# Deformable convolution on one core: in the last batch every second interpolated tile is added up by TensorE

## The chip, the core and the metric

The kernel runs on one core of a Trainium2 chip. The metric is the device time of one execution in microseconds (us). The engines are TensorE (PE, its weight loads are shown apart as PEld), VectorE (DVE), ScalarE (ACT), GpSimd (POOL) and SyncE (SP); 16 DMA engines move data between HBM and the on-chip memory (SBUF), and TensorE writes its results to PSUM.

## The reference

The input is x with 8 images of 256 channels and 64 x 64 pixels, all float32. Two layers follow each other, each with a residual:

```
x = x + L0(gn(x))        # attention in a 3x3 neighbourhood with dynamic kernels, projection
x = x + L1(gn(x))        # modulated deformable 3x3 convolution
```

The change touches L1 alone. For every pixel and every one of the 9 taps a small convolution gives an offset and a mask. The sampled value is a bilinear mix of four corners with the mask folded in, and a 256 x 256 matrix for each tap contracts the channels:

```
v = samp(y0, x0) * ((1-ly)*(1-lx)) + samp(y0, x0+1) * ((1-ly)*lx)
  + samp(y0+1, x0) * (ly*(1-lx)) + samp(y0+1, x0+1) * (ly*lx)
v = v * mask
out = einsum('bckhw,ock->bohw', v, w)
```

## The kernel before, in words

**Tiles of the convolution.** An image is cut into 8 chunks of 512 pixels (8 rows). A unit is one chunk with one tap, 72 units an image. A unit has 4 tiles of 128 pixels, taken as 2 pairs, so an image has 144 pairs or 288 tiles (`PAIRS` = 144). Tiles are numbered through all images as `a`, pairs as `M = b * PAIRS + m`, and `a = 2 * M` or `2 * M + 1`. For each tile the engines do this:

- POOL (L762) gathers 128 rows of 1024 floats from a table in HBM into `G[a % 10]`. Each row holds the four corners of a pixel, 256 channels each. The gather waits until VectorE is done with tile `a - 10` (L761, `lerp[2]`).
- The first corner is scaled by its weight in place: ACT at L1131 in the stretches in which the front part of the next image runs its attention layer and in the last image, otherwise DVE at L1394.
- DVE adds the other three corners, each with one multiply-add (`scalar_tensor_tensor`): L1407 takes corners 0 and 1 into `V[a % 6]`, L1414 adds corner 2 and then corner 3. The two tiles of a pair alternate, so a pair is 6 instructions. Before them DVE waits until PE has turned pair `M - 3` (L1396).
- PE (L988) turns the tile, pixels on partitions to channels on partitions, by 4 transposes of 128 x 128 a pair, into one PSUM bank. It waits for `lerp[2]` (L985).
- ACT (L1142) copies the bank to `VT[U % 2]`, which holds a whole unit.
- PE (L781, `contract`) multiplies `VT` by the tap's weights into the two accumulators `CV[0]` and `CV[1]` (PSUM): 2 matmuls of 512 columns each time, once a pair (first half of the output channels of unit u - 1 at the second pair, second half of unit u - 2 at the first pair).
- After the ninth tap of a chunk DVE (L1198) adds each accumulator to the residual in `R`, SP stores `R` and loads the next one. PE waits for that add before it writes the accumulator again (L777).

**Order.** The order of the work is one written list (`order_of_steps`), and every engine runs its own share of the list in that order; semaphores alone tie the engines. While image b is convolved, the front part of image b + 1 (attention, projection, offsets, table) is laid between the pairs. The last image has no front part beside it. For a pair m the list has: lerp m (DVE), turn m - 1 (PE contracts, then transposes; ACT evacuates; DVE adds a residual where one is due), the gathers of two tiles, scale m + 2 (ACT). So ACT's evacuation of pair m - 1 stands in its queue before the scales of pair m + 2.

**Buffers and counters.** `E[0..5]` are six buffers of 1024 floats for the front part's products and table rows; the last image's convolution does not use them. `lerp[0]`, `lerp[1]` and `lerp[2]` count the tiles after their first, second and third multiply-add. `act_scale` counts ACT's scales, and `scale_counts` works out for each tile which count it has to wait for.

Of the kernel before, what the change touches and what calls it, by code (L numbers as in the profile page):

```python
# [13 lines left out]
P = 128  # L14
# [413 lines left out]
    return [(0, slot, n)] + ([(n, 0, 4 - n)] if n < 4 else [])  # L428


def scale_counts(steps):


    out, n = {}, {True: 0, False: 0}
    for s in steps:
        if s[0] == "scale":
            for i in range(2):
                n[s[3]] += 1
                out[2 * (s[1] * PAIRS + s[2]) + i] = (s[3], n[s[3]])
    return out  # L440


def build(nc, x, wqk, wv, wn, wkx, bkg, alpha, beta, wproj, woff, boff, wconv,
# [1 line left out]
    NB = x.shape[0]  # L445
    steps = order_of_steps(NB)
    banks, prods = rotations(steps)
    scaled = scale_counts(steps)
    ctx = ExitStack()
    with ctx:  # L450
        def sb(name, shape, dt=F32):
# [181 lines left out]
        def rows_of(g, i):  # L633

            n = len(table_blocks(g % NCH)[i])
            return E[prods.place["tt", g, i // 2]][:, CH * (i % 2):CH * (i % 2) + C * n]

        def norm_parts(j, b):

            if j == 1:  # L640
                return 2 + b, mv, gnt, gn2[b % 2]
            part = slice(0, 2) if b == 0 else slice(2, 2 * NB)
            return b, mv1[:, part, :], gnt1[:, :, part], gn1[:, :, part]
# [93 lines left out]
        @block.gpsimd  # L737
        def _(e):
            e.wait_ge(d_first, 16 * NFIRST)
            e.partition_broadcast(s_ab[:, :], row[0:1, 0:36]).then_inc(bcast, 1)  # L740
            e.partition_broadcast(s_bo[:, :], row[0:1, 36:63]).then_inc(bcast, 1)
            e.partition_broadcast(s_al[:, :], row[0:1, 63:65]).then_inc(bcast, 1)

            for s in steps:
                kind = s[0]
                if kind == "gather":
                    b, lo, hi = s[1:]
                    for n in range(lo, min(hi, 2 * PAIRS)):
                        u, i = divmod(n, 4)
                        c, t = unit(u)  # L750
                        a = 2 * PAIRS * b + n
                        col = column(b, c, i, t)
                        if n == 0:
                            e.wait_ge(d_zero, 64)
                            e.wait_ge(st1_done, 16 * NB)
                            for k in range(NE_BUF):
                                need_rows(e, k, NCH * (b + 1) - 1)
                        if n % 36 == 0:
                            e.wait_ge(wts, WTS * (b * NCH + c + 1))
                        if a >= NG:  # L760
                            e.wait_ge(lerp[2], a - NG + 1)  # L761
                        e.indirect_dma_start(  # L762
                            G[a % NG][:, :], None, T[b % 2],
                            bass.IndirectOffsetOnAxis(ap=IDX[:, col:col + 1], axis=0)).then_inc(d_g[a % NG], 16)

        @block.tensor
        def _(e):
# [17 lines left out]
            for s in steps:  # L785
# [189 lines left out]
                elif kind == "turn" and s[2] >= 0:  # L975
                    b, m = s[1:]
                    u, pair = divmod(m, 2)
                    M = b * PAIRS + m
                    if u > 1 and pair == 0:
                        contract(1, b, u - 2)  # L980
                    elif u > 0 and pair == 1:
                        contract(0, b, u - 1)
                    use = ("vt", M)
                    need_bank(e, use)
                    e.wait_ge(lerp[2], 2 * M + 2)  # L985
                    for n in range(2):
                        for h in range(2):
                            mm = e.transpose(BK[banks.place[use]][:, 2 * P * h + P * n:2 * P * h + P * n + P],  # L988
                                             V[(2 * M + n) % NV][:, h * P:(h + 1) * P], s_ident[:, :])
                    mm.then_inc(filled(use)[0], 1)  # L990
                elif kind == "conv.end":
                    b = s[1]
                    contract(1, b, UNITS - 2)
                    contract(0, b, UNITS - 1)
                    contract(1, b, UNITS - 1)

        @block.scalar
        def _(e):
# [29 lines left out]
            for s in steps:  # L1028
# [92 lines left out]
                elif kind == "scale" and s[3]:  # L1121
# [5 lines left out]
                    for i in range(2):  # L1127
                        a = 2 * (b * PAIRS + m) + i
                        col = column(b, c, 2 * pair + i, t)
                        e.wait_ge(d_g[a % NG], 16 * (a // NG + 1))  # L1130
                        e.activation(G[a % NG][:, 0:C], G[a % NG][:, 0:C], ACT.Copy,  # L1131
                                     scale=WT[:, col, 0:1]).then_inc(act_scale, 1)
                elif kind == "turn" and s[2] >= 0:
                    b, m = s[1:]
                    M = b * PAIRS + m
# [10 lines left out]
        def _(e):  # L1146
# [53 lines left out]
            for s in steps:  # L1200
# [182 lines left out]
                elif kind == "lerp":  # L1383
# [24 lines left out]
                                               ALU.mult, ALU.add).then_inc(lerp[0], 1)  # L1408
                    for q in (2, 3):
                        for a, gt, vt, col in pairs:  # L1410
                            e.wait_ge(lerp[q - 2], a + 1)
                            if q == 2 and a % 2 == 1:
                                e.wait_ge(lerp[1], a)  # L1413
                            e.scalar_tensor_tensor(vt[:, :], gt[:, q * C:(q + 1) * C], WT[:, col, q:q + 1], vt[:, :],  # L1414
                                                   ALU.mult, ALU.add).then_inc(lerp[q - 1], 1)
                elif kind == "turn" and s[2] >= 0:
# [83 lines left out]
```

## Time and profile before

| | |
|---|---|
| time before, median of 3 runs | 5265.98 us (5261.78 to 5272.94) |
| the profiled execution's own time | 5259.85 us |
| its span, first to last instruction | 5258.0 us |
| PE busy | 4852.3 us, 92% of the span |
| DVE busy | 4391.8 us, 84% |
| ACT busy | 2248.3 us, 43% |
| POOL busy | 2266.2 us, 43% |
| mean granted TensorE clock | 0.978 of full speed |

A row of a group of instructions names the line, the engine, the operation, the tiles as written<-read, the shapes, and the count; after the bar stand the busy time in us, the mean duration in ns, and the idle time of the engine just before such instructions with what ended it. In a timeline a row is one or more like instructions in a run: start, duration of the whole run, and in brackets the idle time before. Matmuls are pipelined and the profile models their ends. DMA is the busy share of the 16 DMA engines.

### The profile page before, as it was taken

The numbers are of one execution on the slowest core, as the hardware profiler recorded it, in microseconds if no ns is written. First come the engines' busy times: TensorE is split into PE (matmuls) and PEld (weight loads), VectorE is DVE, ScalarE is ACT, GpSimd is POOL, SyncE is SP. The second block draws the span as 40 slices with busy tenths as digits, with TensorE's granted clock in tenths as the row PEclk, the third lists the DMA queues.
The fourth block names the chain that finished last, engine by engine and source line by source line (L and its number), as shares of the span: only waits on it lengthen the run. The fifth ranks groups of instructions, "written<-read, shape, count | busy, mean of one in ns | idle before, by whom it ended". The sixth has DMA issues, their size and how long they took to land. (4 is left out here: it accounts for less than half of the span.)

```text
span 5258.0 us, 79746 instructions
## 1 busy us (share of the span) xinstructions
PE 4852.3 (92%) x26576; PEld 2634.5 (50%) x26576; DVE 4391.8 (84%) x11226; ACT 2248.3 (43%) x5360; POOL 2266.2 (43%) x2311
## 2 busy tenths in 40 slices
PE   7878998999999999999999999899999999998787
PEld 4545554555544555455544555455554555543343
DVE  5748888788997888888898888888888788988888
ACT  2244444344443444434444444434444344443444
POOL 0004444444444444444454444444444444445665
PEclk9989999999999999999999999999999999999899
DMA  5437788877797778977888787888789878798998
GB/s 168 146 135 243 256 277 315 278 260 275 265 345 258 268 268 275 327 252 272 273 295 311 256 276 269 302 287 278 258 275 318 276 261 273 266 326 323 358 365 313
DMA packets 493249, 1451.46 MB, mean 276 GB/s; under 512 B 47524, under 2 KB 117548, under 8 KB 492588
## 3 DMA queue, kind: packets, MB, share of 16 engines
q0 software_dynamic: 331776, 1208.11, 66.5%
q1 hardware_dynamic: 161068, 238.27, 12.9%
q8 instruction: 216, 3.54, 0.3%
q14 instruction: 189, 1.55, 0.1%
HBM read 1309.60 MB, written 136.59 MB: 275 GB/s over the span
## 5 line engine op out<-in xcount | busy, mean ns | idle before, releaser
L762 POOL DMA_INDIRECT G<-table,IDX x2304 | 2265.3, 983 | 2952.7 <-DVE V L1414 2123.4
L781 PE MATMUL ps<-VT,s_wconv 128*128 128x512 f32 x4608 | 2283.0, 619 | 97.7 <-issue 53.6
L1414 DVE SCALAR_TENSOR_TENSOR V<-G,WT,V 128x256 f32<-128x256 f32 x4608 | 2019.0, 479 | 122.9 <-DVE V L1414 2.7
L1142 ACT ACTIVATE VT<-ps 128x512 f32<-128x512 f32 x1152 | 686.9, 596 | 2430.9 <-PE ps L988 1894.4
L781 PEld LDWEIGHTS ps<-VT,s_wconv 128*128 128x128 f32 x4608 | 827.5, 194 | 921.2 <-issue 877.0
L1407 DVE SCALAR_TENSOR_TENSOR V<-G,WT 128x256 f32<-128x256 f32 x2304 | 1007.0, 478 | 234.6 <-ACT G L1131 97.7
L988 PEld LDWEIGHTS ps<-s_ident,V 128*128 128x128 f32 x4608 | 574.2, 143 | 736.2 <-issue 731.5
L1162 DVE TENSOR_TENSOR E<-ps,s_band 128x512 f32<-128x512 f32 x1024 | 649.4, 681 | 271.6 <-PE ps L843 194.7
L1131 ACT ACTIVATE G<-G,WT 128x256 f32<-128x256 f32 x1836 | 825.2, 498 | 26.7 <-DMA G<-table,IDX 16.4
L988 PE MATMUL ps<-s_ident,V 128*128 128x128 f32 x4608 | 705.5, 276 | 75.8 <-DVE V L1414 57.4
L819 PE MATMUL ps<-XN,s_wqk 128*128 128x512 f32 x1024 | 488.2, 605 | 19.5 <-ACT XN L1044 17.7
L843 PE MATMUL ps<-QB,KP 64*128 64x256 f32 (+2 forms) x2944 | 298.9, 340 | 4.5 <-ACT ACX L1006 3.8
L822 PE MATMUL ps<-s_wv,XN 128*128 128x292 f32 x1024 | 293.3, 416 | 0.0
L843 PEld LDWEIGHTS ps<-QB,KP 64*128 64x128 f32 x2944 | 236.3, 188 | 82.1 <-issue 67.9
L819 PEld LDWEIGHTS ps<-XN,s_wqk 128*128 128x128 f32 x1024 | 178.1, 191 | 180.0 <-issue 156.6
L911 PE MATMUL ps<-E,VP 128*64 128x64 f32 (+2 forms) x3008 | 252.1, 317 | 10.2 <-DVE E L1162 6.7
L924 PE MATMUL ps<-ACX,s_wproj 128*128 128x512 f32 x512 | 241.1, 596 | 2.7 <-ACT ACX L1006 1.4
L955 PE MATMUL ps<-KP,s_woff 128*32 128x512 f32 x2048 | 239.9, 603 | 0.0
L822 PEld LDWEIGHTS ps<-s_wv,XN 128*128 128x128 f32 x1024 | 180.1, 190 | 57.4 <-issue 20.3
L911 PEld LDWEIGHTS ps<-E,VP 128*64 128x64 f32 x3008 | 169.0, 139 | 77.5 <-issue 22.2
L1006 ACT ACTIVATE ACX<-ps 128x168 f32<-128x168 f32 (+1 forms) x384 | 111.8, 401 | 185.2 <-PE ps L911 106.3
L1095 ACT ACTIVATE KP<-X,gn 128x64 f32<-128x64 f32 (+1 forms) x352 | 170.9, 568 | 0.6 <-DVE gn L1259 0.4
(101 smaller groups left out, 2668.6 us busy)
## 6 DMA issues: line engine op xcount, KB each, us to landing
table<-E SPq DMA_DIRECT2D x256, 256.0 KB
G<-table,IDX POOLq DMA_INDIRECT x2304
X<-in_x SPq DMA_DIRECT2D x64, 512.0 KB
x<-X SPq DMA_DIRECT2D x64, 512.0 KB, 5.5
R<-x SPq DMA_DIRECT2D x64, 512.0 KB
out<-R SPq DMA_DIRECT2D x64, 512.0 KB
G<-in_x SPq DMA_DIRECT2D x56, 512.0 KB, 4.1
s_wconv<-in_wconv SPq DMA_DIRECT2D x1, 2304.0 KB, 8.6
```

Source lines behind the costliest of these rows:

```text
L762: e.indirect_dma_start(G[a % NG][:, :], None, T[b % 2], bass.IndirectOffsetOnAxis(ap=IDX[:, col:col + 1], axis=0)).then_inc(d_g[a % NG], 16)
L781: mm = e.matmul(CV[oh][:, :], s_wconv[:, h, t, oh * P:(oh + 1) * P], VT[U % 2][:, h, :], start=(t == 0 and h == 0), stop=(t == 8 and h == 1))
L819: mm = e.matmul(bank[:, :], s_wqk[:, h, n * P:(n + 1) * P], XN[:, h, :], start=(h == 0), stop=(h == 1))
L822: mm = e.matmul(bank[:, 0:C + 36], XN[:, h, (n - 4) * P:(n - 3) * P], s_wv[:, h, :], start=(h == 0), stop=(h == 1))
L843: mm = e.matmul(to, k_view(g + t // 4)[part, hp, P * (t % 4):P * (t % 4) + P], QB[g % 2][part, hp, W * lo:W * hi], start=True, stop=True)
L911: mm = e.matmul(BK[banks.place[use]][64 * (h % 2):64 * (h % 2) + 64, W * lo:W * hi], VP[:, (4 * g + t) % NVT, 64 * h:64 * h + 64], E[prods ...
L988: mm = e.transpose(BK[banks.place[use]][:, 2 * P * h + P * n:2 * P * h + P * n + P], V[(2 * M + n) % NV][:, h * P:(h + 1) * P], s_ident[:, :])
L1131: e.activation(G[a % NG][:, 0:C], G[a % NG][:, 0:C], ACT.Copy, scale=WT[:, col, 0:1]).then_inc(act_scale, 1)
L1142: e.activation(VT[U % 2][:, :, 2 * P * pair:2 * P * (pair + 1)], BK[banks.place[use]][:, :].rearrange("p (h n) -> p h n", h=2), ACT.Copy). ...
L1162: e.tensor_tensor(two_rows(E[prods.place[use[0], use[1], use[3]]][:, :], *to), two_rows(BK[banks.place[use]][:, :], 0, 4, 2), band, ALU.mu ...
L1407: e.scalar_tensor_tensor(vt[:, :], gt[:, C:2 * C], WT[:, col, 1:2], gt[:, 0:C], ALU.mult, ALU.add).then_inc(lerp[0], 1)
L1414: e.scalar_tensor_tensor(vt[:, :], gt[:, q * C:(q + 1) * C], WT[:, col, q:q + 1], vt[:, :], ALU.mult, ALU.add).then_inc(lerp[q - 1], 1)
```

## The change

In the last image, of each pair the second tile (odd `a`) is no longer mixed down to one tile. DVE makes two half sums: the upper one, corners 0 and 1, in `V[a % 6]` as before, and a lower one, corners 2 and 3, in a free buffer `E[M % 6]`. For the lower one ACT scales corner 2 too, in place. PE adds the halves while it turns the tile: instead of one transpose for each 128 channels it runs two matmuls against the identity that accumulate in PSUM. The even tile of the pair stays as it was, and images 0 to 6 stay as they were. The waits on `lerp[1]`, `lerp[2]` and `act_scale` count by the new order.

```diff
+    def two_sums(a):
+        return a % 2 == 1 and a >= 2 * PAIRS * (NB - 1)
+    def lerped_by(a):
+        return a + 2 if a % 2 == 0 and two_sums(a + 1) else a + 1
+    def third_by(a):
+        return a + 1 - sum(two_sums(n) for n in range(2 * PAIRS * (NB - 1), a + 1))
...
+        def lower(M):
+            return E[M % NE_BUF][:, 0:C]
...  POOL, before a gather
-                            e.wait_ge(lerp[2], a - NG + 1)
+                            e.wait_ge(lerp[2], lerped_by(a - NG))
...  PE, turn
-                            mm = e.transpose(BK[banks.place[use]][:, 2 * P * h + P * n:2 * P * h + P * n + P],
-                                             V[(2 * M + n) % NV][:, h * P:(h + 1) * P], s_ident[:, :])
+                            to = BK[banks.place[use]][:, 2 * P * h + P * n:2 * P * h + P * n + P]
+                            a = 2 * M + n
+                            if two_sums(a):
+                                e.matmul(to, V[a % NV][:, h * P:(h + 1) * P], s_ident[:, :], start=True, stop=False)
+                                mm = e.matmul(to, lower(M)[:, h * P:(h + 1) * P], s_ident[:, :],
+                                              start=False, stop=True)
+                            else:
+                                mm = e.transpose(to, V[a % NV][:, h * P:(h + 1) * P], s_ident[:, :])
...  ACT, scale
+                        if two_sums(a):
+                            e.activation(G[a % NG][:, 2 * C:3 * C], G[a % NG][:, 2 * C:3 * C], ACT.Copy,
+                                         scale=WT[:, col, 2:3]).then_inc(act_scale, 1)
...  DVE, lerp
                     for q in (2, 3):
                         for a, gt, vt, col in pairs:
-                            e.wait_ge(lerp[q - 2], a + 1)
                             if q == 2 and a % 2 == 1:
-                                e.wait_ge(lerp[1], a)
+                                e.wait_ge(lerp[1], third_by(a - 1))
+                            if two_sums(a):
+                                if q == 2:
+                                    e.wait_ge(act_scale, scaled[a][1] + 1)
+                                    e.scalar_tensor_tensor(lower(M)[:, :], gt[:, 3 * C:4 * C], WT[:, col, 3:4], gt[:, 2 * C:3 * C],
+                                                           ALU.mult, ALU.add).then_inc(lerp[2], 1)
+                                continue
+                            e.wait_ge(lerp[q - 2], a + 1 if q == 2 else third_by(a))
                             e.scalar_tensor_tensor(vt[:, :], gt[:, q * C:(q + 1) * C], WT[:, col, q:q + 1], vt[:, :],
                                                    ALU.mult, ALU.add).then_inc(lerp[q - 1], 1)
```

`scale_counts` adds one to ACT's count after each such tile.

## Rows read from the trace of the kernel before

**Rows 1.** The page's 40 slices of the span: granted clock and traffic.
```profile
PEclk9989999999999999999999999999999999999899
GB/s 168 146 135 243 256 277 315 278 260 275 265 345 258 268 268 275 327 252 272 273 295 311 256 276 269 302 287 278 258 275 318 276 261 273 266 326 323 358 365 313
```

**Rows 2.** Timeline of PE: first transposes of the last image, and its last ones.
```profile
4810.26 1.08 PE L988 MATMUL ps<-s_ident,V 128*128 128x128 f32 x4 [3.44 <-DVE V L1414]
...
5248.35 0.63 PE L988 MATMUL ps<-s_ident,V 128*128 128x128 f32 x4 [0.40 <-DVE V L1414]
```

**Rows 3.** Groups of instructions by line and shape, window 4810 to 5250 us.
```profile
L781 PE MATMUL ps<-VT,s_wconv 128*128 128x512 f32 x567 | 295.8, 647 | 63.4 <-issue 37.5 <-DVE R L1198 21.2 <-ACT VT L1142 4.7
L762 POOL DMA_INDIRECT G<-table,IDX x278 | 279.4, 1005 | 156.3 <-issue 80.1 <-DVE V L1414 76.1
L1414 DVE SCALAR_TENSOR_TENSOR V<-G,WT,V 128x256 f32<-128x256 f32 x573 | 251.2, 479 | 15.3 <-DVE V L1414 0.5
L1131 ACT ACTIVATE G<-G,WT 128x256 f32<-128x256 f32 x282 | 129.6, 500 | 23.2 <-DMA G<-table,IDX 12.8 <-issue 10.0
L1407 DVE SCALAR_TENSOR_TENSOR V<-G,WT 128x256 f32<-128x256 f32 x286 | 125.8, 481 | 49.2 <-issue 29.1 <-ACT G L1131 9.5 <-DVE V L1414 0.8
L988 PE MATMUL ps<-s_ident,V 128*128 128x128 f32 x576 | 93.7, 288 | 25.2 <-DVE V L1414 14.6 <-issue 10.5
L1198 DVE TENSOR_TENSOR R<-ps,R 128x512 f32<-128x512 f32 x14 | 9.6, 683 | 1.0 <-remote 1.0
```

**Rows 4.** Timeline of DVE in the last image: two pairs that follow without a gap.
```profile
5229.07 0.88 DVE L1407 SCALAR_TENSOR_TENSOR V<-G,WT 128x256 f32<-128x256 f32 x2
...
5231.81 0.88 DVE L1407 SCALAR_TENSOR_TENSOR V<-G,WT 128x256 f32<-128x256 f32 x2
```

**Rows 5.** Timeline of PE and ACT where PE has no gap.
```profile
5213.52 1.88 PE L781 MATMUL ps<-VT,s_wconv 128*128 128x512 f32 x4
...
5217.40 0.60 PE L988 MATMUL ps<-s_ident,V 128*128 128x128 f32 x4
...
5217.84 1.88 PE L781 MATMUL ps<-VT,s_wconv 128*128 128x512 f32 x4
...
5218.04 0.60 ACT L1142 ACTIVATE VT<-ps 128x512 f32<-128x512 f32 x1 [0.71 <-issue]
```

**Rows 6.** Timeline of PE in image 6, short float32 matmuls with full weights.
```profile
4746.66 0.97 PE L972 MATMUL ps<-s_selo,LS 128*128 128x27 f32 x8
4747.48 1.11 PE L781 MATMUL ps<-VT,s_wconv 128*128 128x512 f32 x2
```

**Rows 7.** Timelines of PE, ACT and DVE in one stall of the last image.
```profile
5031.55 0.63 PE L988 MATMUL ps<-s_ident,V 128*128 128x128 f32 x4 [0.40 <-issue]
...
5034.29 0.63 PE L988 MATMUL ps<-s_ident,V 128*128 128x128 f32 x4 [0.40 <-DVE V L1414]
...
5039.98 0.60 ACT L1142 ACTIVATE VT<-ps 128x512 f32<-128x512 f32 x1 [5.07 <-remote]
5040.47 0.90 ACT L1131 ACTIVATE G<-G,WT 128x256 f32<-128x256 f32 x2
5040.62 3.78 PE L781 MATMUL ps<-VT,s_wconv 128*128 128x512 f32 x4 [5.71 <-issue]
5041.10 0.88 DVE L1407 SCALAR_TENSOR_TENSOR V<-G,WT 128x256 f32<-128x256 f32 x2 [2.59 <-ACT G L1131]
```

**Rows 8.** Waits in window 4810 to 5250 us: total, times, longest.
```profile
ACT VT L1142 <- remote: 111.9, 36, 6.4
ACT VT L1142 <- PE ps L988: 82.6, 58, 6.8
```

**Rows 9.** Busy time by stretch: us, PE, PEld, DVE, ACT, POOL, clock, DMA share, GB/s.
```profile
4810.00:5250.00 440.00, 354.56 (x1143) 173.55 (x1144) 372.68 (x873) 200.09 (x426) 279.42 (x278) 0.91 0.94 350
...
5100.00:5110.00 10.00, 10.00 (x39) 5.32 (x38) 9.31 (x23) 5.88 (x13) 7.05 (x8) 0.98 0.97 355
5110.00:5120.00 10.00, 6.70 (x25) 3.14 (x24) 8.45 (x21) 3.43 (x8) 7.16 (x8) 1.00 1.03 405
```

More of the change, by code:

```diff
@@ L428, in runs, with scale_counts @@
     return [(0, slot, n)] + ([(n, 0, 4 - n)] if n < 4 else [])
-def scale_counts(steps):
+def scale_counts(steps, two_sums):
     out, n = {}, {True: 0, False: 0}
@@ L437, in scale_counts @@
             for i in range(2):
+                a = 2 * (s[1] * PAIRS + s[2]) + i
                 n[s[3]] += 1
-                out[2 * (s[1] * PAIRS + s[2]) + i] = (s[3], n[s[3]])
+                out[a] = (s[3], n[s[3]])
+                if two_sums(a):
+                    assert s[3]
+                    n[True] += 1
     return out
@@ L447, in build @@
     banks, prods = rotations(steps)
-    scaled = scale_counts(steps)
+    def two_sums(a):
[4 more added lines that the diff above has]
+        return a + 1 - sum(two_sums(n) for n in range(2 * PAIRS * (NB - 1), a + 1))
+    scaled = scale_counts(steps, two_sums)
     ctx = ExitStack()
@@ L1410, in _ @@
                         for a, gt, vt, col in pairs:
-                            e.wait_ge(lerp[q - 2], a + 1)
                             if q == 2 and a % 2 == 1:
-                                e.wait_ge(lerp[1], a)
+                                e.wait_ge(lerp[1], third_by(a - 1))
+                            if two_sums(a):
+                                if q == 2:
[4 more added lines that the diff above has]
+                            e.wait_ge(lerp[q - 2], a + 1 if q == 2 else third_by(a))
                             e.scalar_tensor_tensor(vt[:, :], gt[:, q * C:(q + 1) * C], WT[:, col, q:q + 1], vt[:, :],
```

## The prediction

> **What bounds the kernel now.** The change touches only the last image's convolution, so I first look where that lies and what paces it. The page's slices show that the last tenth differs from the rest: the traffic is highest there, 313 to 365 GB/s, and the granted clock of TensorE is mostly full before, with few slices below [rows 1]. The timeline then gives the stretch itself: from the first transposes of the last image at 4810.26 us to its last at 5248.35 us, 438.1 us for 143 steps from pair to pair, 3.06 us a pair [rows 2]. Everything behind 5248.35 (the last contractions, two adds, a store) is the same after the change, and so is everything ahead of 4810.26.
>
> Next, the pace of each engine in that stretch. DVE: two pairs in a row start at 5229.07 and 5231.81, 2.74 us for six multiply-adds, so 0.457 us each [rows 4]. 143 x 2.74 = 392 us, and the 14 adds at L1198 of 0.68 us make 10 [rows 3]: 402 us of 438. DVE is the pace-maker, and 36 us of stalls lie on top. The idle time before L1407 (49.2 us) and L1414 (15.3 us), part of it pipeline gaps, is of that size [rows 3]. PE: without a gap a pair takes (5217.84 - 5213.52) / 2 = 2.16 us [rows 5]. 143 x 2.16 = 309 us, so PE has 129 us to spare. Of these 63.4 + 25.2 = 89 us are idle [rows 3], and the rest is clock: the mean of 0.91 [rows 9], with levels of full and half speed (2.4 and 1.2 GHz), means 18% of 440 us at half speed, which loses 40 us of work. 89 + 40 = 129, so the account closes. POOL follows: 278 gathers of 1.005 us, with 76.1 us of its idle time ended by DVE [rows 3]. The DMA engines are close behind: share 0.94 at 350 GB/s over the whole stretch, 1.03 at 405 GB/s in a full one [rows 9].
>
> The last view is one stall, read across three engines [rows 7]. PE's transposes of a pair start at 5031.55. Where all is well ACT's evacuation starts 0.64 us after the transposes do (5217.40, 5218.04) [rows 5]. Here it starts at 5039.98, 8.4 us after, though PE's records show nothing slow. Its idle time of 5.07 us is ended by "remote", a semaphore whose event the profile can't name [rows 7]. Waits of this kind total 111.9 us in 36 cases in this stretch, and those ended by L988 another 82.6 us [rows 8]; the short ones do no harm, as ACT has slack. In the long one everything hangs on it: ACT's scales stand behind the evacuation (5040.47), DVE waits for them until 5041.10 (2.59 us), and PE, which needs the evacuated tile for its next contraction, idles 5.71 us to 5040.62 and then runs four instructions in 3.78 instead of 1.88 us, at half clock [rows 5, 7]. So a stall costs DVE 2.6 us and PE 5.7 + 1.9 = 7.6 us. 36 us of DVE stalls at 2.6 are about 14 of them. The Trainium skill, "Perfetto Trace Analysis" (Per-instruction lifecycle), says that for TensorE the reported end is an estimate and that the semaphore goes out later, when PSUM has acknowledged; the late evacuation behind punctual records [rows 7] agrees, and it is why I take ACT's start and not PE's end for when a tile was there.
>
> **The change, part by part.** There are 144 changed tiles, one a pair.
>
> DVE: six multiply-adds become five. 5 x 0.457 = 2.28 us a pair, minus 0.46 [rows 4]. The new instruction has the old one's shape. Over 143 pairs DVE then needs 327 + 10 = 337 us, so it leaves the path; the 0.46 us is a gain only until something else is late.
>
> ACT: one more scale a pair at 0.50 us (129.6 us for 282 are 0.46 each as they overlap) [rows 3]. An evacuation plus three scales is 0.5 + 3 x 0.46 = 1.9 us in a pair of 2.8. Hidden; but it lengthens the loop evacuation, scales, multiply-adds, transposes by 0.46 us, as the multiply-adds shorten it by 0.46. Net nothing.
>
> PE: two of four transposes go, four matmuls come. The transposes start 0.11 us apart ((5217.84 - 5217.40) / 4), one instruction each [rows 5]. A float32 matmul is two instructions: a pair contracts with two matmuls, and the rows show four L781 instructions in 2.16 - 0.44 = 1.72 us, 0.43 each for 512 columns [rows 5]. So four matmuls are eight instructions, six more a pair. No row has a float32 matmul of 128 columns with 128 x 128 weights. By columns it is 0.43 x 128 / 512 = 0.11 us. If the weight load binds, the nearest row has eight instructions with such weights and only 27 columns in 4747.48 - 4746.66 = 0.82 us, 0.10 each [rows 6]. Both ends agree at 0.10 to 0.11; the far upper end, were nothing pipelined, is the mean duration of 0.288 [rows 3]. No gain is possible here. I take 0.11: 6 x 0.11 = 0.66 us, a pair goes from 2.16 to 2.82 us, and PE needs 143 x 2.82 = 403 us. In the first microseconds the clock is at half (four transposes took 1.08 us against 0.60) [rows 2, 5]; PE now pays for that, some 5 us. PE is the new pace-maker at 408 us. It passes DVE's 402 by a hair.
>
> A rule speaks against this. The Trainium skill, "TensorE: Matmul & The Clock Gate" (Terms), calls the transpose mode four times faster for float32. By it a matmul of 128 columns would cost 4 x 0.11 = 0.44 us and not the 0.22 of my sum. It is a rival below.
>
> POOL and DMA: nothing is added. The gather's wait for the odd tile ends a little earlier, since its last multiply-add is now the fourth of five. POOL has run at 2.74 us a pair at DVE's pace [rows 4] with idle time left [rows 3], so 2.82 is within its reach. Bytes: 350 GB/s x 438 us are 153 MB. At 350 / 0.94 = 372 GB/s they need 412 us, at 405 GB/s 379 us [rows 9]. So at 408 us the DMA engines are full or nearly so. SP's transfers stay.
>
> New waits: DVE's lower sum waits for ACT's second scale. Behind it are one multiply-add and the next pair. ACT runs ahead by two pairs, so it is free, unless an evacuation is late, and then DVE waits at L1407 already.
>
> **Stalls.** The sum hangs on them. Before, a stall cost the pace-maker 2.6 us; now it costs PE the full 7.6. Nothing catches up afterwards: PE had 0.6 us a pair to do so and has none. With n stalls the stretch is 408 + 7.6 n us, and the break-even against 438 is n = 4. Today n is 14. What starts one? From 5100 to 5110 PE has no gap (busy 10.00), DMA share is 0.97, and all is well. From 5110 to 5120 PE is busy only 6.70 and the DMA share is 1.03: a stall [rows 9]. In images 0 to 6 PE is gapless most of the time, traffic reaches 345 GB/s, and the clock is rarely below full [rows 1]. I read it so that an evacuation comes late when PE runs in bursts with gaps while the DMA engines are full. With PE as pace-maker the gaps go (0.40 us before each group of transposes in [rows 7]), and DMA demand falls by 3% (2.74 to 2.82). This is an inference from few rows. I take n = 2: 408 + 15 = 423 us, 15 us less than 438. The profiled execution took 5259.85 us, 1.85 more than its span and 6 less than the median of 5265.98; I lay the difference on the median: 5251 us. Its own range, n from 0 to 4, is 5236 to 5266.
>
> **Rivals.**
> First, and on the other side: the stalls stay. They come from full DMA engines and not from PE's gaps, and PE pays for each. For it: share 1.03 in the stall, and demand falls by 3% only [rows 9]. Against it: 0.97 without one. It decides from n = 4. With n = 7 the stretch is 461 us, plus 23: 5289 us; with all 14 it is 514, plus 76: 5342 us. Since a longer stretch thins the traffic, the lower one is likelier, about 5295.
> Second, the gathers bound it. DMA at 372 GB/s needs 412 us and with refills after each residual's store and load some 430: minus 8, 5258 us. For it: share 0.94 over all. Against it: L1131 waited for gathers only 12.8 us [rows 3].
> Third, matmul instructions of 128 columns cost twice what I take: 8 x 0.22 + 0.22 + 1.72 = 3.70 us a pair, 143 x 3.70 + 5 = 534 us, plus 96: 5362 us. It is the skill's factor of four. Against it: 0.43 for 512 columns, and 0.10 for 27 [rows 5, 6].
>
> **Chances.** Forecast 0.45, stalls stay 0.28, gathers bound 0.22, dear matmuls 0.05. What a measurement of this kernel can tell from no change is about 0.2%, 10.5 us. The forecast lies beyond that on the fast side with about 0.75 of its chance (n up to 2), the second rival with 0.4, the first with a little at n = 4 to 5 within it: faster 0.43, same 0.25, slower 0.32. For 8 in 10 the range runs from 5232 (no stalls, and a few us from the add handovers) to 5305, which takes in the first rival up to n = 9 and leaves out the third.
>
> **What would show it.** In the last image: DVE's pair of five in 2.28 us; L988 as 10 instructions a pair 0.11 apart; PE's gapless pair at 2.82; PE idle down from 89 us to under 25 and the clock above 0.97; long evacuation waits nearly gone. If the clock stays near 0.9 and PE still has idle stretches of 5 us, the first rival holds and the prediction is wrong. If PE waits for DVE still, the sum for DVE is wrong. If ACT's L1131 waits for gathers by tens of microseconds, it is the second.

## The result, and the profile after

The changed kernel takes 5291.56 us (median of 7 runs, 5283.48 to 5300.87), the kernel before 5265.98 us (7 runs beside them, 5254.76 to 5272.94). The ratio is 1.0046, interval 1.0036 to 1.0056: slower by 24 us by the ratio and by 26 us by the medians, where 15 us faster was forecast. The profiled execution took 5295.5 us, with a span of 5293.7 (before 5258.0).

The page's slices of the changed kernel, as in [rows 1]:

```profile
PEclk9989999999999999999999999999999999999999
GB/s 169 144 141 236 267 270 329 272 262 272 264 341 253 261 279 280 313 259 281 267 294 293 272 260 277 315 282 261 273 268 329 266 259 270 275 316 330 340 334 295
```

The clock of the last tenth has risen to 9 throughout, as forecast, and yet the traffic there is lower, at most 340 GB/s where it was 365: the last image has become longer. PE's timeline gives its ends, as in [rows 2]:

```profile
4815.09 0.66 PE L1017 MATMUL ps<-s_ident,V 128*128 128x128 f32 x2 [2.98 <-DVE V L1451]
...
5283.35 0.38 PE L1017 MATMUL ps<-s_ident,V 128*128 128x128 f32 x2
```

From 4815.09 to 5283.35 that is 468.3 us for 143 steps, against 438.1. The last image took 30 us more, and everything ahead of it took 5 us more. Next the groups of that stretch (window 4815 to 5284 us), as in [rows 3], and the row of the same window, as in [rows 9]. L1013 and L1014 are the two matmuls of the odd tile:

```profile
L803 PE MATMUL ps<-VT,s_wconv 128*128 128x512 f32 x564 | 276.3, 613 | 44.3 <-ACT VT L1173 34.5 <-issue 9.8
L1451 DVE SCALAR_TENSOR_TENSOR V<-G,WT,V 128x256 f32<-128x256 f32 x286 | 136.9, 479 | 0.0
L1438 DVE SCALAR_TENSOR_TENSOR V<-G,WT 128x256 f32<-128x256 f32 x286 | 125.9, 481 | 143.1 <-ACT G L1159 72.1 <-issue 60.8 <-DVE V L1451 3.9
L1013 PE MATMUL ps<-s_ident,V 128*128 128x128 f32 x574 | 114.6, 282 | 0.0
L1014 PE MATMUL ps<-s_ident,E 128*128 128x128 f32 x574 | 114.2, 281 | 0.2 <-issue 0.2
L1447 DVE SCALAR_TENSOR_TENSOR E<-G,WT 128x256 f32<-128x256 f32 x143 | 69.4, 485 | 5.1
L1017 PE MATMUL ps<-s_ident,V 128*128 128x128 f32 x288 | 57.5, 283 | 3.0 <-DVE V L1451 3.0
```
```profile
4815.00:5284.00 469.00, 424.41 (x2000) 271.98 (x2001) 316.40 (x729) 249.87 (x566) 279.51 (x278) 0.96 0.89 329
```

DVE now idles 143 us ahead of its first multiply-add, and PE has become the busy engine: 424.4 of 469 us, at a clock of 0.96 (0.91 before). PE's idle time fell from 88.6 to 47.3 us. What was to fall far lower are the waits for late evacuations, as in [rows 8]:

```profile
ACT VT L1173 <- remote: 116.0, 29, 7.5
ACT VT L1173 <- PE ps L1014: 67.4, 58, 5.8
```

They have not: 116.0 and 67.4 us, against 111.9 and 82.6. One such stall on PE, ACT and DVE, as in [rows 5, 7]:

```profile
5041.52 1.88 PE L803 MATMUL ps<-VT,s_wconv 128*128 128x512 f32 x4
5043.24 0.38 PE L1017 MATMUL ps<-s_ident,V 128*128 128x128 f32 x2
...
5044.35 1.88 PE L803 MATMUL ps<-VT,s_wconv 128*128 128x512 f32 x4
...
5049.70 3.54 PE L803 MATMUL ps<-VT,s_wconv 128*128 128x512 f32 x4 [2.35 <-issue]
```
```profile
5049.05 0.60 ACT L1173 ACTIVATE VT<-ps 128x512 f32<-128x512 f32 x1 [3.25 <-remote]
...
5050.74 0.58 ACT L1173 ACTIVATE VT<-ps 128x512 f32<-128x512 f32 x1
```
```profile
5050.17 0.88 DVE L1438 SCALAR_TENSOR_TENSOR V<-G,WT 128x256 f32<-128x256 f32 x2 [2.85 <-ACT G L1159]
```

The first three PE rows are a pair without a gap: contraction 1.72 us, then ten turning instructions in 1.11 us, 2.83 us in all (forecast: 2.82). The tile turned from 5043.24 is evacuated at 5049.05, 5.8 us later, though the last instruction of the turn started at 5044.24. The trace also holds the semaphore's own event: it comes at 5049.02, 4.5 us after the recorded end of that instruction, and ACT starts 0.03 us behind it. In the stall of [rows 7] the event comes 7.8 us after the recorded end and ACT again starts 0.03 us behind it. So it is TensorE's semaphore that is late, and not ACT. PE had gone on for one pair and then stands for 2.35 us and runs its next four instructions in 3.54 us and not 1.88, at half clock (0.54 granted from 5049.7 to 5053.0): 2.35 + 1.66 = 4.0 us lost on the engine that now sets the pace. The account of the stretch: 143 x 2.83 = 405 us, plus 47 us of PE's idle time, plus 16 for half clock and the rest, makes 468.

So the theory after the result: the pace came out as forecast, and the late evacuations, which I took for a consequence of PE's gaps, stayed. The experiments ask what makes them late (full DMA engines, or PE's own work), and what each part of the change does by itself.

### The profile page after: what moved, and what is told of

Its sections match the earlier page's. It is cut to its first block and busy times, and to the rows that moved or that the text cites. A ratio compares the mean times of both kernels' runs of the same rounds, so it can differ in the third digit from the quotient of the medians.

```text
span 5293.7 us, 81474 instructions
## 1 busy us (share of the span) xinstructions
PE 4925.7 (93%) x27440; PEld 2735.3 (52%) x27440; DVE 4340.0 (82%) x11082; ACT 2301.1 (43%) x5504; POOL 2265.4 (43%) x2311
## 2 busy tenths in 40 slices
DMA packets 493256, 1451.58 MB, mean 274 GB/s; under 512 B 47524, under 2 KB 117548, under 8 KB 492588
## 5 line engine op out<-in xcount | busy, mean ns | idle before, releaser
L1451 DVE SCALAR_TENSOR_TENSOR V<-G,WT,V 128x256 f32<-128x256 f32 x4320 | 1907.0, 480 | 36.0
L1173 ACT ACTIVATE VT<-ps 128x512 f32<-128x512 f32 x1152 | 686.6, 596 | 2419.3 <-PE ps L1017 1852.6
L1017 PEld LDWEIGHTS ps<-s_ident,V 128*128 128x128 f32 x4320 | 544.3, 142 | 687.4 <-issue 683.0
L1017 PE MATMUL ps<-s_ident,V 128*128 128x128 f32 x4320 | 669.5, 275 | 47.5 <-DVE V L1451 40.8
```

What stands on the lines that cost most here:

```text
L1017: mm = e.transpose(to, V[a % NV][:, h * P:(h + 1) * P], s_ident[:, :])
L1173: e.activation(VT[U % 2][:, :, 2 * P * pair:2 * P * (pair + 1)], BK[banks.place[use]][:, :].rearrange("p (h n) -> p h n", h=2), ACT.Copy). ...
```

## The experiments

Ratios are to the kernel before, run beside them. For each trace two numbers say where the time lies: when ACT's first evacuation of the last image starts (all that is ahead of it), and how long it is from there to the last evacuation (the last image). Before: 4811.4 and 437.6 us. After: 4817.6 and 467.1 us. A further 9 us follow in each trace (6.5 in those with the contraction halved).

**First group: parts of the change, and the traffic halved.** In half_gather_before and half_gather_after the last image's gather brings the upper two corners only; the lower two are left over from the image before, and every instruction stays:

```diff
-                            G[a % NG][:, :], None, T[b % 2],
+                            G[a % NG][:, 0:2 * C] if b == NB - 1 else G[a % NG][:, :], None, T[b % 2],
```

> The kernel before; in the last image each gather brings only the first 512 of the 1024 floats of a row, so corners 2 and 3 there are left over from the image before. Same number of gathers, rows and instructions, half the bytes. Theory F (an evacuation comes late because the DMA engines are full): late evacuations (over 3 us after the transposes) all but vanish, the last image's stretch of 438 us falls to DVE's 402, about 36 us or 0.7% faster than before. Theory P (they come from POOL's gather instructions or from TensorE itself, whatever the bytes): the stretch stays at about 438 us and the time within 0.2%.

> The changed kernel with the same halved gathers in the last image. Theory F: the stretch falls from 468 us to TensorE's 408, so some 36 us (0.7%) faster than the kernel before and no slower than the halved kernel before by more than 6 us. Theory P: it stays at about 468 us, 0.5% slower than before.

pe_alone is the kernel before with the odd tile turned by two matmuls of the same half, so that only PE's work is added:

```diff
-                            mm = e.transpose(BK[...], V[...][:, h * P:(h + 1) * P], s_ident[:, :])
...  to and half stand for the two arguments above
+                            if n == 1 and b == NB - 1:
+                                e.matmul(to, half, s_ident[:, :], start=True, stop=True)
+                                mm = e.matmul(to, half, s_ident[:, :], start=True, stop=True)
+                            else:
+                                mm = e.transpose(to, half, s_ident[:, :])
```

> TensorE's part of the change alone: DVE mixes every tile down as before, and in the last image TensorE turns each odd tile by two float32 matmuls against the identity for each 128 channels (the second writes the same again). If the loss comes from TensorE's added 0.66 us a pair and stalls that it can no longer absorb, the whole loss is here: the stretch is 465 to 475 us, 0.45 to 0.7% slower than before. If the loss came from ACT's extra scale or the new order on DVE, this one is within 0.2% of before (its gapless pace is 2.82 against DVE's 2.74, 11 us).

dve_act_alone is the changed kernel with PE turning the upper sum alone (the lower one is left out of the result):

```diff
-                                e.matmul(to, V[a % NV][:, h * P:(h + 1) * P], s_ident[:, :], start=True, stop=False)
-                                mm = e.matmul(to, lower(M)[:, h * P:(h + 1) * P], s_ident[:, :],
-                                              start=False, stop=True)
+                                mm = e.transpose(to, V[a % NV][:, h * P:(h + 1) * P], s_ident[:, :])
```

> The part of DVE and ACT alone: two sums as in the change, but TensorE turns only the upper one by a transpose, so the lower half of the odd tiles is left out of the last image's result. TensorE needs 2.16 us a pair, DVE 2.28. Theory F says that the DMA engines are next: the pace then is limited by 153 MB at 372 to 405 GB/s, 379 to 412 us, with late evacuations still there: stretch 400 to 430 us, 10 to 35 us (0.2 to 0.7%) faster than before. If the late evacuations set the pace by themselves and not DVE, the stretch stays near 438 us.

Measured: half_gather_before 5151.59 us, 1.0002 (0.9993 to 1.0012). half_gather_after 5132.92, 0.9966 (0.9953 to 0.9978). pe_alone 5161.03, 1.0019 (1.0009 to 1.0029). dve_act_alone 5115.14, 0.9931 (0.9915 to 0.9948).

No expectation allowed for what stood beside them: the kernel before itself took 5150.99 us, 115 us less than in the first comparison (by the traces 70 of them ahead of the last image and 39 in it). In these traces TensorE's late semaphores are absent. The waits that end by "remote" show it best. Over the whole span of the kernel before in the first comparison they are:

```profile
ACT VT L1142 <- remote: 198.2, 62, 6.4
ACT ACX L1006 <- remote: 69.6, 21, 5.3
DVE V L1407 <- remote: 22.1, 7, 4.4
```

With four small rows more these are 329 us. In half_gather_before and pe_alone, whose images 0 to 6 are those of the kernel before, there is no such row at all. Nor does any image 0 to 6 hold an evacuation over 3 us behind the recorded end of its transposes (before: 26 of them, and 42 in the last image). dve_act_alone has 25 of 3.0 to 3.9 us in its last image, but of another kind: the semaphore is punctual there, and ACT comes to it late from scales that waited for gathers. The semaphore events say the same. In each of the 14 traces of this document that have no "remote" row, every recorded event of TensorE comes within 0.1 us of the recorded end of its matmul. In the other six 115 to 223 of some 3,900 come over 2 us late (before: 171, up to 9.2 us), and some 600 events are missing there; VectorE's and ScalarE's show no such lag. So the first group could not tell where late ones come from, and the question of full DMA engines stayed open. What it shows without them: pe_alone's last image takes 405.4 us and half_gather_before's 398.8, with PE gapless in the one and at DVE's pace in the other. And the change seemed to gain: half_gather_after is 0.34% faster than the kernel before. dve_act_alone gained 36 us with a last image of 388 us, a little more than expected (10 to 35 us, 400 to 430 us).

**Second group: the changed kernel again, and the order of two waits.** The diff holds a second edit. In every image the odd tile's multiply-add of corner 2 (its second multiply-add; the expectations call it the third) has two waits, and `wait_ge(lerp[1], ...)` now stands ahead of `wait_ge(lerp[0], ...)`, where it was behind it. wait_swap is the kernel before with this alone:

```diff
                         for a, gt, vt, col in pairs:
-                            e.wait_ge(lerp[q - 2], a + 1)
                             if q == 2 and a % 2 == 1:
                                 e.wait_ge(lerp[1], a)
+                            e.wait_ge(lerp[q - 2], a + 1)
```

> The kernel before with one thing of the change: ahead of the third multiply-add of the odd tile DVE's wait on lerp[1] is written before the wait on lerp[0], in all images. In the trace of before the two third multiply-adds of a pair start 582 ns apart, in that of the changed kernel 514. Theory: this 68 ns a pair counts in all images, 8 x 144 x 0.068 = 78 us of DVE's time, of which images 0 to 6, where other work shares DVE, give some 3 us each (607 to 604 us between first and last evacuation) and the last image 10: 20 to 33 us (0.4 to 0.65%) faster where late evacuations are absent. Rival: DVE's time there is hidden, and the kernel stays within 0.1% of before.

last_image_only is the changed kernel with the old order in images 0 to 6:

```diff
+                            if b < NB - 1:
+                                e.wait_ge(lerp[q - 2], a + 1)
+                                if q == 2 and a % 2 == 1:
+                                    e.wait_ge(lerp[1], a)
+                                e.scalar_tensor_tensor(vt[:, :], ...).then_inc(lerp[q - 1], 1)
+                                continue
```

> The changed kernel, but in images 0 to 6 DVE's waits stand in the order of the kernel before, so only the last image differs from before. Theory: TensorE's pace of 2.83 us a pair against DVE's 2.745 costs 143 x 0.085 = 12 us less the handovers: 5 to 12 us (0.1 to 0.25%) slower than before where late evacuations are absent, some 30 us slower where they are there. If it is faster than before, the gain of the changed kernel there does come from the two sums.

after_again is the changed kernel without an edit:

> The changed kernel as it is, once more. In the four runs so far the kernel before took 5151 us where it took 5266 in the first comparison, and no kernel with whole gathers and TensorE at 2.82 us a pair showed an evacuation later than 3 us after the transposes. Theory C (the late evacuations belong to the chip or its memory and not to the kernel): where the kernel before takes about 5151 us this one has none either, its last stretch is 405 us (TensorE at 2.83 us a pair), and the kernel is 10 to 25 us faster than before, not 24 slower; where the kernel before takes about 5266 us it is 0.3 to 0.6% slower again. Theory K (they belong to this kernel): the stretch is near 468 us and the kernel 0.3 to 0.6% slower anywhere.

every_second_pair makes two sums in every second pair only:

```diff
-        return a % 2 == 1 and a >= 2 * PAIRS * (NB - 1)
+        return a % 4 == 3 and a >= 2 * PAIRS * (NB - 1)
```

> The changed kernel with two sums in the odd tile of every second pair only (72 tiles and not 144). TensorE: 2.16 + 0.33 = 2.49 us a pair on average, DVE: 5.5 multiply-adds and the shorter wait, about 2.48. Theory D (next are the DMA engines): 1.05 MB a pair at 405 to 412 GB/s is 2.56 to 2.6 us, with the residual's 8.4 MB 390 us: stretch 388 to 395 us, 25 to 35 us faster than before where late evacuations are absent. If TensorE and DVE set the pace, 360 us and 60 us faster. With late evacuations: not slower than before by more than 10 us.

Measured beside 5149.65 us of the kernel before, again with no "remote" row (start of the last image and its length behind each): after_again 5130.23, ratio 0.9961 (0.9947 to 0.9975), 4717.6 and 404.0. wait_swap 5119.25, 0.9937 (0.9921 to 0.9954), 4717.2 and 391.9. last_image_only 5152.37, 1.0006 (0.9996 to 1.0015), 4738.9 and 402.6. every_second_pair 5117.3, 0.9936 (0.9919 to 0.9952), 4714.9 and 391.2. The kernel before is at 4741.0 and 398.8 (half_gather_before's trace).

The pieces add up. The waits' order gains 24 us ahead of the last image and 7 in it (31, measured 30.4). The two sums bring a last image of 404.0 or 402.6 us where DVE's pace gave 398.8 with the old order and 391.9 with the new. So the changed kernel gains 23 ahead of the last image and loses 5 in it: 18, measured 19.4. last_image_only lost 3 us, less than the 5 to 12 expected; the other three came out within what was expected. The DVE timelines of image 4 show where the order acts. First half_gather_before, then wait_swap, with six multiply-adds of a pair each:

```profile
3000.45 0.87 DVE L1407 SCALAR_TENSOR_TENSOR V<-G,WT 128x256 f32<-128x256 f32 x2
3001.24 1.86 DVE L1414 SCALAR_TENSOR_TENSOR V<-G,WT,V 128x256 f32<-128x256 f32 x4
```
```profile
3001.05 0.88 DVE L1407 SCALAR_TENSOR_TENSOR V<-G,WT 128x256 f32<-128x256 f32 x2
3001.84 1.79 DVE L1414 SCALAR_TENSOR_TENSOR V<-G,WT,V 128x256 f32<-128x256 f32 x4
```

The four take 1.79 and not 1.86 us, in nearly each pair of images 0 to 6. The changed kernel has 1.79 too, last_image_only 1.86.

The windows of the last image show what bounds it, columns as in [rows 9]. In this order: half_gather_before, after_again, wait_swap, dve_act_alone:

```profile
4735.00:5134.00 399.00, 336.08 (x1128) 160.42 (x1127) 371.01 (x870) 196.17 (x423) 289.25 (x278) 0.96 0.70 204
```
```profile
4717.00:5122.00 405.00, 404.02 (x2001) 261.66 (x2000) 316.25 (x728) 254.53 (x567) 276.71 (x278) 1.00 0.98 380
```
```profile
4717.00:5109.00 392.00, 341.60 (x1139) 163.69 (x1138) 372.04 (x871) 210.15 (x425) 280.64 (x278) 0.95 1.00 393
```
```profile
4717.00:5105.00 388.00, 336.69 (x1141) 170.50 (x1142) 323.78 (x724) 255.77 (x564) 277.06 (x277) 0.96 1.00 396
```

In after_again PE is busy 404 of 405 us: it is the bound. With half the traffic (204 GB/s) the kernel before takes the same time (1.0002): its gathers are hidden. In dve_act_alone neither PE (337 us) nor DVE (324) binds, and the DMA share is 1.00. The waits of the same windows, first dve_act_alone, then wait_swap:

```profile
ACT G L1157 <- DMA G<-table,IDX: 121.9, 152, 1.7
DVE V L1436 <- ACT G L1157: 45.5, 127, 1.2
```
```profile
ACT G L1131 <- DMA G<-table,IDX: 119.3, 202, 2.5
DVE V L1407 <- ACT G L1131: 3.1, 8, 0.6
```

ACT waits for gathers in both, but only in dve_act_alone does DVE wait for ACT in turn (45.5 us). In wait_swap it hardly does (3.1 us): its pairs follow 2.68 us apart, 143 x 2.68 = 383 us and 10 for the adds, so DVE's own pace makes its 392 us. The gathers set the pace in dve_act_alone at 388 us, and in part in every_second_pair at 391 us, with PE busy 367 us and DVE waiting 21.6 us for ACT. That floor rests on these waits; no run halves the gathers of these two.

**Third group: with late evacuations again.** before_again and after_third are the two kernels without an edit, no_third_wait the kernel before without the odd tile's `wait_ge(lerp[1], a)`, second_pair_no_wait the same edit on every_second_pair (there the wait counts by `third_by(a - 1)`).

```diff
                             e.wait_ge(lerp[q - 2], a + 1)
-                            if q == 2 and a % 2 == 1:
-                                e.wait_ge(lerp[1], a)
```

> The kernel before, word for word, for its trace. Theory C: where it takes 5150 us, TensorE's semaphores are punctual (no evacuation over 3 us after the transposes), images 0 to 6 take 607 us each and the last one 402 (DVE's pace of 2.745 us a pair and the adds). If the chip is one like that of the first comparison it takes about 5266 us and some 40 of the last image's 144 evacuations are over 3 us late.

> The changed kernel word for word beside it. Theory C: where the kernel before takes 5150 us, 0.3 to 0.5% faster; where it takes 5266, 0.3 to 0.6% slower, with late evacuations in both.

> The kernel before without DVE's wait on lerp[1] ahead of the odd tile's third multiply-add (DVE runs its instructions in order, and the tile's own wait on lerp[0] stays). The 582 ns between the two third multiply-adds of a pair (514 with the waits swapped) should fall to 396, the pitch of the others: DVE then needs 2.56 us a pair. Images 0 to 6: a further 118 ns a pair beside the 68 of the swap, which gave 3.3 us an image, so 8 to 10 us an image. The last image: DMA engines bound it at 390 us. In all 75 to 90 us (1.4 to 1.7%) faster than before. Rival: the wait costs nothing more than the swap already gives, 0.6%.

> The changed kernel with two sums in every second pair only, and without that wait on lerp[1] in all images. If the DMA engines bound the last image at 390 us, the two sums bring nothing there and this kernel equals the one without the wait within 0.1%. If DVE still has a part in it, it is up to 5 us faster.

On this chip the kernel before took 5237.1 us, and the "remote" waits were back: 142.9 us at L1142 in before_again, 164.0 at L1173 in after_third. Measured beside it: before_again 5235.57, 1.0000 (0.9986 to 1.0013), 4802.6 and 428.8. after_third 5258.31, 1.0041 (1.0025 to 1.0057), 4789.4 and 457.7. no_third_wait 5236.15, 1.0002 (0.9991 to 1.0012), 4777.1 and 441.0. second_pair_no_wait 5240.61, 1.0005 (0.9992 to 1.0017), 4773.7 and 452.5.

The first comparison's result is thus repeated, and so is its place: the last image of the changed kernel is 28.9 us longer (29.5 then). Windows of before_again and after_third:

```profile
4802.00:5231.00 429.00, 355.85 (x1139) 174.11 (x1139) 372.50 (x872) 200.12 (x425) 280.22 (x278) 0.91 0.95 359
```
```profile
4789.00:5247.00 458.00, 423.24 (x1998) 271.12 (x1997) 315.36 (x727) 250.72 (x566) 277.34 (x278) 0.96 0.91 336
```

no_third_wait was expected 75 to 90 us faster and is not faster at all. It saves DVE a wait in each pair. By its trace it gains 25.5 us ahead of the last image and loses 12 in it, though PE has no more to do than before; the two profiled executions lie 13 us apart (5228.84 and 5242.22) where the medians are 0.6 us apart, so small differences between single traces of this group say little. A faster DVE brought nothing back in this group. second_pair_no_wait, with the two sums in half of the pairs, has a last image 11.5 us longer than no_third_wait (452.5 and 441.0), with medians 4 us apart. That fits PE's added work as the part that costs, but no run gave PE's part alone in such a session: pe_alone, dve_act_alone and wait_swap met none.

**Fourth and fifth group: traffic or PE's work.** These were to tell apart what makes them late, by halving the gathered bytes (the edit of the first group) or the contraction of the last image, on two chips, the second being the one of the third group:

```diff
-                for h in range(2):
+                for h in range(1 if b == NB - 1 else 2):
...  the stop flag moves to the half that is left
```

> The kernel before with halved gathers in the last image (corners 2 and 3 of the last image are left over from the image before), on another chip. Where the kernel before takes over 5200 us: Theory F (full DMA engines make TensorE's semaphores late): punctual in the last image, its stretch falls from about 430 to 400 us, the kernel 25 to 40 us faster than before. Theory T (TensorE's own load does): the stretch stays over 425 us. Where the kernel before takes 5150 us it only repeats 399 us.

> The changed kernel with halved gathers in the last image. Where the kernel before takes over 5200 us: theory F: the stretch falls from about 460 to 404 us, TensorE's own pace. Theory T: it stays over 440 us, since TensorE is as busy as before.

> The kernel before, where in the last image each contraction takes only the first 128 input channels (half of its matmuls are left out), so TensorE needs 1.30 and not 2.16 us a pair; the gathers are whole. Where the kernel before takes over 5200 us: theory F: the late semaphores stay, the stretch is 420 to 440 us. Theory T: they vanish, the stretch falls to DVE's 400 us.

> The kernel before with halved gathers in the last image (corners 2 and 3 of the last image are left over from the image before). Where the kernel before takes over 5200 us: theory F: punctual in the last image, stretch from about 430 to 400 us, 25 to 40 us faster than before. Theory T: the stretch stays over 425 us.

> The changed kernel with halved gathers in the last image. Where the kernel before takes over 5200 us: theory F: the stretch falls from about 460 to 404 us. Theory T: it stays over 440 us.

> The kernel before with half of each contraction left out in the last image, gathers whole. Where the kernel before takes over 5200 us: theory F: the late semaphores stay, stretch 420 to 440 us. Theory T: they vanish, stretch 400 us.

Measured beside 5149.46 us: 5148.36 (ratio 0.9999, 0.9987 to 1.0010), 5130.8 (0.9965, 0.9952 to 0.9979) and 5146.74 (0.9994, 0.9983 to 1.0005). Then beside 5151.39 us: 5150.57 (0.9997, 0.9986 to 1.0008), 5130.42 (0.9960, 0.9944 to 0.9976) and 5147.37 (0.9993, 0.9982 to 1.0004). No trace of either group has a "remote" row, even on the chip that had shown them before. For their own question they are inconclusive, as no expectation with a kernel before of over 5200 us could be put to the test. They do show that the condition belongs neither to the kernel nor for good to a chip. With punctual evacuations they also settle the two paces. The contraction halved leaves PE with 229 us of 399 in the kernel before, and the last image stays at 398.5 to 398.7 us: DVE sets it. The traffic halved leaves the changed one at 403.9: PE does. And half_contract3 has both conditions of the prediction at once, PE's gaps and full DMA engines. Its PE timeline, then its window:

```profile
4990.13 0.63 PE L988 MATMUL ps<-s_ident,V 128*128 128x128 f32 x4 [1.26 <-DVE V L1414]
4990.59 1.02 PE L781 MATMUL ps<-VT,s_wconv 128*128 128x512 f32 x2
4992.88 0.63 PE L988 MATMUL ps<-s_ident,V 128*128 128x128 f32 x4 [1.26 <-DVE V L1414]
```
```profile
4735.00:5134.00 399.00, 229.10 (x850) 108.55 (x848) 371.40 (x870) 210.30 (x424) 288.51 (x278) 0.94 1.00 388
```

PE stands 1.26 us in each of these pairs and the DMA share is 1.00, and no wait ends by "remote". A DMA share of 1.00 does not say either that the gathers set the pace: the length is that of half_gather_before at 0.70, and DVE does not wait for a scale.

## Why the prediction was wrong

Right were the terms of PE and DVE. A turn is ten instructions 0.11 us apart, a gapless pair 2.83 us (2.82 forecast), the last image without late evacuations 404 us where I had 408, with PE as pace-maker; before it is 399 where I had 402. ACT's extra scale is hidden: last_image_only, with the whole of the edit, is 3 us slower than the kernel before, and not more than pe_alone, without the scale (10 us). The clock rose to 0.96, and to 1.00 in after_again. The second rival (430 us by the gathers) fell: two versions with whole gathers need 388 and 391 us. The third fell too. A float32 matmul of 128 columns costs two transposes' time: 0.22 against 0.11 us in the ten instructions from 5043.24 to 5044.35. The rule in "TensorE: Matmul & The Clock Gate" (Terms) of the Trainium skill gives the transpose a factor of four for float32; here it is two.

The step that failed is the one under "Stalls": "I read it so that an evacuation comes late when PE runs in bursts with gaps while the DMA engines are full ... I take n = 2". PE's gaps ahead of its transposes went, and the evacuations more than 3 us late in the last image went from 42 to 48 (from 32 to 24 in the second session, before_again and after_third), nowhere near from 14 to 2. Conversely, in half_contract3 and wait_swap PE has its gaps and the DMA share is 1.00, and no wait ends by "remote". Neither gaps nor full DMA engines, nor both, suffice. Where late semaphores occur, they do go with traffic: cut into stretches of 10 us, the last images of the six traces have 285 of 932 events over 2 us late where the DMA share is 0.9 or more, and 24 of 277 where it is less. That is a correlation; no run with late ones changed the traffic. The forecast was +6 us of pace and -21 of stalls. Measured in the last image: +5 of pace (398.8 to 404.0), and +24 because late evacuations cost the changed kernel 63 us (467.1 - 404.0) and the kernel before 39 (437.6 - 398.8). The second session with late ones gives 54 and 30 (457.7 - 404.0, 428.8 - 398.8), +24 again. Per evacuation over 3 us late that is 0.9 us in the kernel before in both sessions, and 1.3 and 2.2 us in the changed one: what rose in both sessions is the price, as forecast from PE's lost slack; the number rose in one and fell in the other. The forecast's price was too high (7.6 us of PE; the stall shown cost 4.0) and its number far too low. The first rival held with its side. Its time came close (5289 us, stretch 461; measured 5291.56 and 468), but by luck: it had 7 stalls at 7.6 us. Its cause, full DMA engines, is not shown either.

A second step was missing. I read "images 0 to 6 stay as they were" off my own account of the diff and priced the moved wait at nothing. By wait_swap it is worth 0.63% with punctual evacuations, more than all else in the change. In the first comparison it can't be seen: images 0 to 6 came out 6 us later there, and 13 us earlier in after_third than in before_again. Between traces with late evacuations the same stretch of the same kernel differs by 9 us (4811.4, 4802.6).

So the sign depends on a condition outside the kernel: +0.46% and +0.41% with late evacuations, -0.39% without. In the latter the two sums have no part; alone (last_image_only) they are at +0.06%, which is no difference clear of noise (0.9996 to 1.0015). The best versions with punctual evacuations are wait_swap and every_second_pair, 5119 and 5117 us against 5150 and 5130; they differ by less than the interval. With late ones none of the versions run beat the kernel before; wait_swap itself met no such session.

What stays open: what makes TensorE's semaphores late, and which part of the change costs the 24 us where they are. "Perfetto Trace Analysis" (Per-instruction lifecycle) of the Trainium skill says that TensorE's recorded end is an estimate and its semaphore goes out later. The stalls agree: there the evacuation starts 5.8 to 8.4 us behind the start of the turn, and the semaphore's event 4.5 to 7.8 us behind the recorded end. The good pair does not show it: its transposes are recorded from 5217.40 to 5218.00, and ACT starts at 5218.04 [rows 5]. Why one session has 26 of over 3 us in images 0 to 6 and another none, no run here tells, nor is it on record what else the chip did meanwhile.

## What to carry to other kernels

A stall whose releaser the profile can't name isn't to be forecast away from a correlation of two windows: make the forecast with the stalls left as they are, and price them anew for the engine that becomes the pace-maker, as its slack no longer takes them up. Before a wait is called the bound, follow it on: ACT waited 119 us for gathers in wait_swap, but DVE waited only 3 us for ACT. Where a diff reorders waits, count it as an edit of every loop that runs through it, and run it alone. And time the same pair of kernels in more than one session before believing half a per cent: here the sign turned.

## What the hardware showed unexpectedly

- The same program took 5237 to 5266 us in two sessions and 5149 to 5151 us in four others, and the changed kernel, word for word the same, 5292 and 5258 or 5130 us. The changed kernel's traces after and after_again move the same 1451.58 MB and differ by TensorE's late semaphores: 363 us of "remote" waits in the first and none in the second. One chip showed both.
- Two waits ahead of one DVE instruction cost by their order: 1.86 or 1.79 us for the four multiply-adds of a pair, and without the second wait, by no_third_wait's DVE timeline:

```profile
3003.52 1.66 DVE L1412 SCALAR_TENSOR_TENSOR V<-G,WT,V 128x256 f32<-128x256 f32 x4
```

- The gathers of 4 KB rows reach a DMA share of 1.00 at 393 to 396 GB/s over 390 us (wait_swap, dve_act_alone), with TensorE's semaphores punctual throughout. In half_contract3 the share is 1.00 at 388 GB/s already.
